# A two-layer state-space and expert kernel: the last y sums read from PSUM, the order behind the scans and its idle turns rewritten, expert rows added up by TensorE

## The reference

```python
x = x + _layernorm(_L0_attn_ref(_layernorm(x), ...))   # selective scan, 16 states
x = x + _layernorm(_L0_ffn_ref(_layernorm(x), ...))    # signs of x times signs of a weight
x = x + _layernorm(_L1_attn_ref(_layernorm(x), ...))   # the second selective scan
x = x + _layernorm(_L1_ffn_ref(_layernorm(x), ...))    # 16 experts, top 2, and a shared one
```

```python
scores = jax.nn.softmax(t @ gate_w.T, axis=-1)
weights, indices = jax.lax.top_k(scores, TOP_K)
for e in range(N_EXPERTS):
    w_e = jnp.sum(jnp.where(indices == e, weights, 0.0), axis=-1)
    y = y + _swiglu(t, w1[e], w3[e], w2[e]) * w_e[:, None]
z = _swiglu(t, sw1, sw3, sw2)
return y + z
```

## Time and profile before

| | us |
|---|---|
| median of 3 runs (lowest, highest) | 726.14 (725.17, 728.02) |
| the profiled execution | 727.01 |
| its span, from the first to the last instruction | 725.0 |
| TensorE, weight loads, VectorE, ScalarE, GpSimd busy | 627.7, 534.5, 559.0, 520.5, 443.9 |
| mean granted clock of TensorE | 0.927 of full speed |

### The profile page before, as it was taken

How to read it: one execution, slowest core, us unless ns; L and a number is a source line. 1 busy time by engine, 2 the same in 40 slices (tenths; PEclk the granted TensorE clock), 3 DMA queues, 4 the chain that set the end, 5 groups by cost and what they waited for, 6 DMA issues and landing times.

```text
span 725.0 us, 12906 instructions
## 1 busy us (share of the span) xinstructions
PE 627.7 (87%) x4302; PEld 534.5 (74%) x4303; DVE 559.0 (77%) x1068; ACT 520.5 (72%) x1267; POOL 443.9 (61%) x396
## 2 busy tenths in 40 slices
PE   4758999999994759489999999979899999999950
PEld 2348999999993423389999999977677677777630
DVE  6797999999997895879999999967832544344378
ACT  2959999999997969599999999963543222222425
POOL 0036999999997340369999999980674233333300
PEclk9957999999997869689999999999999999999985
DMA  6032454445440000144545454461122233332163
GB/s 182 5 73 76 143 147 133 143 140 145 135 145 1 0 2 7 42 111 135 160 127 161 135 154 140 133 206 46 66 103 94 88 102 102 108 108 95 64 219 116
DMA packets 57577, 77.83 MB, mean 107 GB/s; under 512 B 8112, under 2 KB 38480, under 8 KB 57520
## 3 DMA queue, kind: packets, MB, share of 16 engines
q1 hardware_dynamic: 53728, 66.75, 31.7%
q0 software_dynamic: 3792, 10.36, 4.0%
HBM read 58.21 MB, written 18.87 MB: 106 GB/s over the span
## 4 chain that ended last, share of the span: by engine, by line
PE 76%; DVE 11%; ACT 9%; DMA 2%; issue 1%; POOL 1%; ACTq 0%; SPq 0%; POOLq 0%; DVEq 0%
PE bank L1135 24%; PE bank L1158 15%; PE bank L1203 12%; PE bank L1137 4%; ACT tok_a L771 3%; PE bank L1048 3%; PE bank L1211 3%; PE bank L1212 3%; PE bank L1154 2%; DVE st L360 2%; DVE rings L740 1%; DVE arena L460 1%; PE bank L1273 1%; PE bank L1060 1%; PE bank L1074 1%
## 5 line engine op out<-in xcount | busy, mean ns | idle before, releaser
L961 POOL TENSOR_TENSOR arena<-arena,rings 128x512 f32<-128x512 f32 x256 | 317.2, 1280 | 23.2 <-DVE arena L557 22.0
L557 DVE TENSOR_TENSOR_SCAN arena<-rings,bank 128x512 f32<-128x512 f32 x256 | 302.1, 1211 | 14.1 <-PE bank L1137 12.3
L1135 PE MATMUL bank<-rings,tok_a 128*128 128x128 f32 x1536 | 217.9, 279 | 4.7 <-ACT rings L871 4.7
L1135 PEld LDWEIGHTS bank<-rings,tok_a 128*128 128x128 f32 x1536 | 196.4, 196 | 5.4 <-issue 5.4
L881 ACT ACTIVATE rings<-arena,a_sb 128x512 f32<-128x512 f32 x256 | 169.7, 709 | 1.1 <-DVE arena L557 1.1
L1158 PE MATMUL bank<-ident,arena 128*128 128x128 f32 x1024 | 152.4, 273 | 1.1 <-POOL arena L961 1.1
L871 ACT ACTIVATE rings<-ident,b_tok 128x128 f32<-128x128 f32 x384 | 124.5, 388 | 0.4 <-ACT tok_a L831 0.4
L1158 PEld LDWEIGHTS bank<-ident,arena 128*128 128x128 f32 x1024 | 119.4, 141 | 2.0 <-POOL arena L961 2.0
L1000 POOL DMA_INDIRECT y_tok<-rings,dest x47 | 45.5, 967 | 85.0 <-DVE rings L701 84.7
L936 ACT ACTIVATE silu<-bank 128x176 f32<-128x176 f32 x47 | 14.9, 318 | 85.7 <-PE bank L1203 85.7
L701 DVE COPY rings<-bank 128x256 f32<-128x256 f32 x47 | 20.0, 425 | 67.2 <-PE bank L1212 67.2
(11 more groups left out here) (170 smaller groups left out, 894.5 us busy)
## 6 DMA issues: line engine op xcount, KB each, us to landing
rings<-c_rows SPq DMA_DIRECT2D x128, 256.0 KB, 3.5
w_sb<-w SPq DMA_DIRECT2D x18, 352.0 KB, 4.3
x_sorted<-zeros SPq DMA_DIRECT2D x47, 128.0 KB, 3.4
rings<-x_sorted SPq DMA_DIRECT2D x47, 128.0 KB, 2.0
arena<-w SPq DMA_DIRECT2D x2, 2048.0 KB, 12.9
residual<-x SPq DMA_DIRECT2D x4, 512.0 KB, 5.8
tok_a<-y_tok SPq DMA_DIRECT2D x4, 512.0 KB, 7.9
w_sb<-y_tok SPq DMA_DIRECT2D x4, 512.0 KB, 9.1
```

The lines of the kernel that those rows point to most:

```text
L557: dve.tensor_tensor_scan(state[:, u % STATE_RING, :], abar[:, u % ABAR_RING, :], bank[u % B_RING][:, :], 0.0, ALU.mult, ALU.add).then_inc( ...
L961: pool.tensor_tensor(s, s, crep[:, k % CREP_RING, :], ALU.mult).then_inc(hc_ready, 1)
L1135: pe.matmul(o, tok_a[:, c, h * P:(h + 1) * P], v_ring[:, s % V_RING, j, 0:P], start=True, stop=True)
```

## The change

- SHARED_FIRST is 14: one more shared chunk ahead of the tiles, two behind.
- `y_last` is gone. Statistics and norm of the last y block read PSUM directly. The orders `first_y`, `first_f`, `last` and `combine` are rewritten. For the second layer's turns the target is banks 0 and 1, and turn 0 waits for the scan's last unit.
- The idle turns have other counts, with 16 new ones before turn 0 and 6 before the shared chunks.
- The picks of blocks 2 and 3 are one step. The second product of `expert_rows` takes the picks expert by expert, so that the copy that reordered its result goes; the multiply by 128 becomes part of the next addition; the first chunk's gated products come before the wait for the sums.
- ScalarE's function tables for silu and for the square root are loaded ahead of the first use.
- The weighted additions are TensorE's: `shared_part` puts `f_moe` into PSUM with the identity, `routed_part` adds each expert row through a diagonal of weights; the 32 diagonals are made by ScalarE (`mix_weights`), the first eight among the shared chunks, the others behind them. Statistics and norm read the sums in PSUM.

The diff, cut to its core:

```diff
-SHARED_FIRST = 13
+SHARED_FIRST = 14
...
+        turn_bank = [work, work, bank[0:2]]
+        mixed_in = [bank[6:8], bank[0:2], bank[2:4], bank[4:6]]
+        mix_diag = arena[:, 0:2 * C * P].rearrange("p (k c d) -> p k c d", k=2, c=C)
...
-        first_y = [("y_stat", 0), ("y_stat", 1), ("y_stat", 2), ("y_add", 0), ("y_last", 3), ("y_add", 1)]
-        first_f = first_y + [("f_stat", 0), ("y_add", 2), ("y_stat", 3), ("f_norm", 0)]
+        first_y = [("y_stat", 0), ("y_stat", 1), ("y_stat", 2), ("y_add", 0), ("y_add", 1), ("y_stat", 3), ("y_add", 2)]
+        first_f = first_y + [("f_stat", 0), ("f_norm", 0)]
         middle = first_f + [step for step in middle if step not in first_f]
-        last = first_y + [("y_stat", 3), ("y_add", 2), ("turn", 0), ("x_stat", 0), ("y_add", 3), ("turn", 1),
-                ("gate", 0), ("x_stat", 1), ("turn", 2), ("gate", 1), ("pick", 0), ("x_stat", 2), ("turn", 3),
-                ("gate", 2), ("pick", 1), ("x_stat", 3), ("gate", 3), ("pick", 2), ("pick", 3), ("x_norm", 0)]
-        combine = [("softmax", 0), ("gates", 1), ("m_add", 0), ("gates", 2), ("m_add", 1), ("gates", C - SHARED_FIRST),
-                   ("m_stat", 0), ("m_stat", 1), ("m_add", 2), ("m_norm", 0), ("m_stat", 2), ("m_norm", 1),
-                   ("m_add", 3), ("m_out", 0), ("m_stat", 3), ("m_norm", 2), ("m_out", 1), ("m_norm", 3),
-                   ("m_out", 2), ("m_out", 3)]
+        last = first_y + [("x_stat", 0), ("turn", 0), ("y_add", 3), ("turn", 1), ("x_stat", 1), ("gate", 0), ("turn", 2),
+                ("x_stat", 2), ("gate", 1), ("pick", 0), ("turn", 3), ("x_stat", 3), ("gate", 2), ("pick", 1),
+                ("gate", 3), ("pick", 2), ("x_norm", 0)]
+        combine = [("softmax", 0), ("gates", 1), ("gates", 2), ("m_stat", 0), ("m_norm", 0), ("m_stat", 1), ("m_norm", 1),
+                   ("m_out", 0), ("m_stat", 2), ("m_norm", 2), ("m_out", 1), ("m_stat", 3), ("m_norm", 3), ("m_out", 2),
+                   ("m_out", 3)]
+        def mix(c):
+            return mixed_in[c // CQ][c % CQ // 2][:, c % 2 * D:(c % 2 + 1) * D]
+        def last_y(c):
+            return ysum_of[(Q - 1) % 2][c % CQ // 2][:, c % 2 * D:(c % 2 + 1) * D]
...
-            def stat(src, q, ready=None, count=0, each=1):
+            def stat(src, q, ready=None, count=0, each=1, y_sum=False, mixing=False):
...
-                    done(dve.bn_stats(st6[:, c, :], src[:, c, :]))
+                    done(dve.bn_stats(st6[:, c, :], last_y(c) if y_sum else mix(c) if mixing else src[:, c, :]))
...
-                        if q == Q - 1:
-                            x_scales(q)
...
-                        stat(tok_a, q, last_y_copied, (l - 1) * 2, 2)
+                        dve.wait_ge(state_free, l * BATCH * UNITS)
+                        stat(tok_a, q, y_sum=True)
...
-                    dve.wait_ge(gate_ready, q + 1)
-                    done(dve.tensor_copy(gates[:, g, 0:E], logits[q]))
+                    if q == 1:
+                        x_scales(Q - 1)
+                    n = 1 if q < 2 else 2
+                    g = slice(q * CQ, (q + n) * CQ)
+                    for b in range(q, q + n):
+                        dve.wait_ge(gate_ready, b + 1)
+                        done(dve.tensor_copy(gates[:, b * CQ:(b + 1) * CQ, 0:E], logits[b]))
...
+            shared_gates(2)
             dve.wait_ge(prefix_ready, 1)
-            done(dve.tensor_copy(chunk_count, work[1][:, 0:C * E].rearrange("p (c e) -> p e c", c=C)))
-            settle()
-            done(dve.tensor_tensor_scan(chunk_end.rearrange("p e c -> p (e c)"), not_first,
-                                        chunk_count.rearrange("p e c -> p (e c)"), 0.0, ALU.mult, ALU.add))
-            shared_gates(2)
+            chunk_count = work[1][:, 0:C * E]
+            done(dve.tensor_tensor_scan(chunk_end.rearrange("p e c -> p (e c)"), not_first, chunk_count, 0.0, ALU.mult, ALU.add))
...
-            done(dve.tensor_scalar(row0[:, :], row0[:, :], float(P), None, ALU.mult))
-            settle()
-            done(dve.tensor_tensor(chunk_end, chunk_end, row0[:, :].unsqueeze(2).to_broadcast([P, E, C]), ALU.add))
+            done(dve.scalar_tensor_tensor(chunk_end, row0[:, :].unsqueeze(2).to_broadcast([P, E, C]), float(P), chunk_end,
+                                          ALU.mult, ALU.add))
...
-                elif name == "m_add":
-                    dve.wait_ge(moe_copied, (q + 1) * CQ)
-                    for j in range(CQ + 1):
-                        for k, c in ((0, q * CQ + j), (1, q * CQ + j - 1)):
-                            if not 0 <= c - q * CQ < CQ:
-                                continue
-                            if k == 0:
-                                dve.wait_ge(y_loaded[q], 16 * 2)
-                            else:
-                                dve.wait_ge(dve_done, steps[0] - (j < CQ))
-                            done(dve.scalar_tensor_tensor(f_moe[:, c, :], y_k[k][:, c, :], weights[:, c, k:k + 1],
-                                                          f_moe[:, c, :], ALU.mult, ALU.add))
-                    settle()
                 elif name == "m_stat":
-                    stat(f_moe, q)
+                    dve.wait_ge(mixed, q + 1)
+                    stat(None, q, mixing=True)
...
+                    y = last_y(c) if name == "y_add" and q == Q - 1 else mix(c) if name == "m_norm" else src[:, c, :]
+                    act.activation(dst[:, c, :], y, ACT.Identity, scale=rstd[:, c:c + 1], bias=shift[:, c:c + 1])\
...
+                    if (name, q, l) == ("x_stat", Q - 1, 2):
+                        act.preload_act_table_set("silu_and_others")
...
-                elif name == "y_last":
-                    act.wait_ge(state_free, l * BATCH * UNITS)
-                    for j in range(2):
-                        act.activation(tok_a[:, q * CQ + 2 * j:q * CQ + 2 * j + 2, :],
-                                       ysum_of[1][j][:, :].rearrange("p (c d) -> p c d", c=2), ACT.Copy).then_inc(last_y_copied, 1)
...
+            def mix_weights(q):
+                if q == 0:
+                    act.wait_ge(weights_ready, 1)
+                    act.wait_ge(ty_ready, TILES)
+                for c in range(q * CQ, (q + 1) * CQ):
+                    for k in range(2):
+                        ins = act.activation(mix_diag[:, k, c, :], ident[:, :], ACT.Copy, scale=weights[:, c, k:k + 1])
+                ins.then_inc(mix_ready, 1)
...
+                    if hi == C and c == lo:
+                        mix_weights(0)
...
+                        if c == C:
+                            act.preload_act_table_set("sqrt_and_others")
...
+            for q in range(1, Q):
+                mix_weights(q)
...
-            idle_turns = {("turn", 1): 14, ("gate", 0): 8, ("turn", 2): 12, ("gate", 1): 8, ("turn", 3): 12, ("gate", 2): 4,
-                          ("gate", 3): 8}
+            idle_turns = {("turn", 0): 16, ("turn", 1): 22, ("gate", 0): 2, ("turn", 2): 6, ("gate", 1): 4, ("turn", 3): 6,
+                          ("gate", 2): 4, ("gate", 3): 10}
...
-                    if l and q == 0:
-                        pe.wait_ge(last_y_copied, l * 2)
+                    if l == 1 and q == 0:
+                        pe.wait_ge(y_normed, C)
+                    if l == 2 and q == 0:
+                        pe.wait_ge(h_ready, 2 * BATCH * UNITS)
...
-                pe.wait_ge(onehot_ready, Q)
-                flat = picked.rearrange("p c e -> p (c e)")
-                pe.matmul(work[0][:, 0:C * E], upper_sb[:, :], flat, start=True, stop=True)
-                pe.matmul(work[1][:, 0:C * E], ones[:, :], flat, start=True, stop=True).then_inc(prefix_ready, 1)
+                pe.wait_ge(onehot_ready, Q - 1)
+                pe.matmul(work[0][:, 0:C * E], upper_sb[:, :], picked.rearrange("p c e -> p (c e)"), start=True, stop=True)
+                pe.matmul(work[1][:, 0:C * E], ones[:, :], picked.rearrange("p c e -> p e c"), start=True, stop=True)\
+                  .then_inc(prefix_ready, 1)
...
+                    if hi == C and c == lo:
+                        shared_part(0)
+                    if hi == C and c == C + 1:
+                        shared_part(1)
...
+            def shared_part(q):
+                for c in range(q * CQ, (q + 1) * CQ):
+                    pe.matmul(mix(c), ident[:, :], f_moe[:, c, :], start=c % 2 == 0, stop=False, skip_group_check=True)
+            def routed_part(q):
+                pe.wait_ge(mix_ready, q + 1)
+                pe.wait_ge(y_loaded[q], 16 * 2)
+                for k in range(2):
+                    for c in range(q * CQ, (q + 1) * CQ):
+                        ins = pe.matmul(mix(c), mix_diag[:, k, c, :], y_k[k][:, c, :], start=False, stop=k == 1,
+                                        skip_group_check=True)
+                ins.then_inc(mixed, 1)
...
+            stay_busy(6, bank[1])
...
+            shared_part(2)
+            routed_part(0)
```

(32 more changed lines are left out.)

3 lines of the change are left out of this document (1 added, 2 removed).

## The result

The changed kernel takes 725.01 us (median of 12 runs, lowest 723.59) against 726.67 us before (12 runs); the ratio is 0.9978, 95% interval 0.9968 to 0.9988. That is 1.7 us faster, where 4.4 were forecast. 725.0 lies inside the range, and the interval holds no 1, but the gain is under the 0.5% that I took for the smallest difference to be told: of a clear gain, little more than a third came. (One of the 12 runs of the changed kernel took 796.43 us in a slower state of the chip, and the ratio leaves it out.) The profiled execution took 725.35 us with a span of 723.5, against 727.01 and 725.0.

The account below looks back on a forecast made before the run. TensorE was taken to bound the middle stages, short VectorE instructions the routing, and a chain of loads, VectorE additions and a cold chunk the tail; -0.2 - 3.5 + 4.0 - 4.7 = -4.4 us, so 721.8 us, range 717.5 to 727.

Parts of the forecast that it names:

- Behind the first scan: First scan's end: dropping the 0.96 us copy of the last y sum gives -0.2 us, ends 1.0 gained and 0.3 lost.
- Turns, gates, picks, routing: Second scan to third shared chunk: no copy, fewer idle turns, shorter VectorE routing; -4.3 us at full clock, -3.5 taken.
- the warm end: Second scan to third shared chunk: with TensorE at full clock that chunk starts near 507.3, not 511.64, -4.3 us.
- Rival (d): Behind the second scan: idle turns, being transposes, do not hold TensorE's clock; up to 727.3 us, chance 0.03.
- I take -3.5, between the two, nearer to the warm end: Up to the third shared chunk: gain taken between -4.3 at full clock and 1.0 with clock falls and a late pick.
- Rival (a): Routing stretch: TensorE's clock falls from gate products or the new idle stretch; gain 1.0, not 3.5, 724.3 us, chance 0.25.
- signs of being wrong: Clock 0.5 within 683 to 712; routed product waiting over 1 us; chunk pitch other than 4.0; tiles starting after 563.
- One more chunk, paid in full: Ahead of the tiles: SHARED_FIRST 13 to 14 costs one chunk-loop pitch, +4.0 us, with POOL's scatters off the path.
- The tail: After the tiles: TensorE's sums replace VectorE's additions; 29.1 us plus 8.0 behind them, 37.1 instead of 41.8, -4.7 us.
- The 0.17 of the prediction: Tail: alternative estimate from the skill's fixed access cycles, four norms reading PSUM are 0.17 us shorter, not 0.4.
- Rival (b): Tail: bound by ScalarE or VectorE, roots and norms queueing behind 24 diagonals; tail 39.5 us, 724.2 us, chance 0.12.
- Rival (c): Tail: TensorE's sums run at half clock after a pause, 36 products at 0.86, +15.5 us, 737 us, chance 0.07.

Follow-up runs that it names:

- e7: Kernel before with only the last y sum's copy removed (statistics and norm read PSUM, second-layer turns in banks 0 and 1): 739.00 against 739.98 us, 0.9987.
- f4: Changed kernel without any idle turns, beside a kernel before of about 727 us: 732.41 us, ratio 1.0080.
- e1: Changed kernel plus 26 idle turns on TensorE ahead of the third shared chunk: 722.21 us, ratio 0.9944.
- e3: Changed kernel with SHARED_FIRST back at 13, so three shared chunks in the tail: 724.59 us, ratio 0.9968.
- f1: Changed kernel with 26 idle turns ahead of the third shared chunk, blocks 0 and 1 added by VectorE, SHARED_FIRST 13: 714.07 us, ratio 0.9821.
- e4: Changed kernel with additions split, blocks 0 and 1 on VectorE, blocks 2 and 3 on TensorE with 16 diagonals: 719.86 us, ratio 0.9900.
- e5: Changed kernel without any idle turns, on the chip where the kernel before took 740.0 us: 741.56 us, ratio 1.0016.
- e8: Changed kernel, 26 idle turns ahead of the third shared chunk, blocks 0 and 1 added by VectorE, SHARED_FIRST 14, chip of 740.0 us: 732.05 us, 0.9891.

## Why the prediction was wrong, step by step

**Behind the first scan**: right. -0.30 measured between the scan's last unit and the first f_turn, -0.2 forecast; e7 has the same with this edit alone.

**Turns, gates, picks, routing**: right in mechanism and size. Chunk 2 starts 4.16 us sooner, and -4.3 was the warm end. The routing's sums reach VectorE 3.0 us sooner behind the scan's last unit (3.2 forecast), and from there to chunk 2 are 5.91 us (5.8 to 5.9 forecast). Gates and first chunk ran at full clock, which is up to 1.7 us of the 4.16. Rival (d), that idle turns do nothing for the clock, does not hold: f4 shows what is lost without them.

**"I take -3.5, between the two, nearer to the warm end": this step failed.** I had named the new idle stretch of 3.2 us between chunks 1 and 2, priced a fall of the clock there at up to 1.75 us, and then took only 0.8 us off the warm end of -4.3. The stretch came (3.25 us) and cost 2.88: eight products 2.43 us longer, the three turns and the first down product behind them the rest. I had taken the price from the old first chunk, which ran cold for only a part of its products; a whole chunk cold is 5.0 us, as the old tail's already said. So the stretch up to chunk 3 gained 1.28 us and not 3.5. Rival (a) named this mechanism, with a chance of 0.25 and a gain of 1.0; e1 takes the idle stretch away and gets 722.2 us. That this is within 0.4 of the forecast is partly luck, since the 1.3 us that the tail fell short (below) are missing there too. Of the signs of being wrong that I had listed, only this came, as a first pitch of the chunk loop of 7.14 us in place of 4.0; I had named no window of the clock between the gates and the loop.

**One more chunk, paid in full**: right, +3.99, and the scatters stayed off the path. That the chunk costs nearly the same in the tail is e3; that it need not, f1.

**The tail**: the mechanism was right, the size was not. Forecast 29.1 + 8.0, measured 29.8 + 8.5, -3.4 in place of -4.7. The 48 products took 20.7 us, as forecast (20.6). The 0.7 lies in the work of the two last shared chunks: the first eight up products took 2.63 us and not 2.37 (0.3), the second group of turns 0.55 and not 0.33 (0.2), and the wait and rounding are the rest. VectorE came to the last sum 0.6 us late, at 715.56 in the chain, as forecast. The 0.5 lies behind that: from there to the end are 7.94 us and not 7.4, of which 0.3 is a norm that gains less from PSUM than the 0.4 I took and 0.2 the last store (2.77 us from VectorE's last addition to the end of the span, 2.56 before). The norms from PSUM in the changed kernel and from SBUF in the one before (the three figures are the least, median and greatest ns of one):

```profile
L769 ACT ACTIVATE rings<-bank,shift,rstd x16: 555/565/572, 705.7 to 719.4; 128x256 f32<-128x256 f32 x16
...
L771 ACT ACTIVATE rings<-rings,shift,rstd x16: 584/586/600, 709.1 to 721.1; 128x256 f32<-128x256 f32 x16
```

That is 565 ns against 586, and four take 1.93 us instead of 2.07, 0.14 less; no run shows the 0.4. The 0.17 of the prediction, an estimate worked out from the Trainium skill ("VectorE: DVE Perf Modes", the section on the TRN2 errata), was the better number. Rival (b), a tail bound by ScalarE or VectorE, does not hold: the diagonals were done at 705.1, TensorE waited 0.6 us in 29.8, and e4, which takes 24 products off TensorE and gives VectorE the additions of two blocks, gained 5.2 us. Rival (c) did not happen: the clock was full until TensorE was done.

Against my own sum, the two errors are 2.2 us before the tiles and 1.3 in the tail, 3.5 of the 4.4. That would leave -0.9, and the two traces have -0.83 behind the point where the edits begin. The medians of the runs say -1.7; the other 0.8 us no run assigns.

## What to carry to other kernels

When work ahead of TensorE gets shorter, look at the pauses that this opens in TensorE's own queue, and price a fallen clock over everything that runs until it comes back, not over one old case. One trace is not enough to say where it falls: the kernel before and e7 had the same wait of 2.60 us and their falls in different chunks. A move of additions from one engine to TensorE is worth only what the other engine bound; here 20.7 us of products replaced 15 us of VectorE for 1 us, and a split over both engines gave 5.2 us more and left room to hide a chunk.

## What the runs showed that I had not expected

A busy TensorE is not one at full clock: in f4 it is busy for 5.00 of 5.00 us at 0.50 during the gate products, and transposes that nobody reads, put before and between them, go with 1.00 and 7.4 us less in the changed kernel. The clock can also fall with no idle stretch in front. In the kernel before TensorE was busy for 14.00 of 14.00 us with turns, idle turns and gate products, and then it fell:

```profile
485.00:499.00 14.00, 14.00 (x131) 14.00 (x129) 9.65 (x69) 6.66 (x16) 2.75 (x5) 1.00 0.54 170
499.00:500.00 1.00, 1.00 (x6) 0.77 (x6) 0.62 (x4) 0.00 (x0) 0.00 (x0) 0.74 0.00 0
```

In e7, with the same counts of idle turns, the clock did not fall there, and in the ten traces with the new counts it did not either. No run settles what decides it.

On the chip of e5 to e8 all kernels, the one before too, took longer (the one before 740.0 us and not 726.8; the three others that ran on both chips 9 to 15 us more). In the trace of e8 the time lies in the shared chunks during GpSimd's scatters. Two rows of its timeline, TensorE and ScalarE:

```profile
546.35 2.71 PE L1235 MATMUL bank<-w_sb,feat_a 128*128 128x352 f32 x4 [6.86 <-issue]
...
552.45 0.41 ACT L938 ACTIVATE silu<-bank,x_scale 128x176 f32<-128x176 f32 x1 [6.59 <-remote]
```

TensorE stood for 6.86 us with nothing that the trace shows as a reason ("issue"), ScalarE for 6.59 until something outside the engines ("remote"), with more such waits around them, the first near 535. TensorE's long one ended at 546.35 with scatters still to come, ScalarE's at 552.45, 2.5 us behind the last of them (548.95 to 549.91); the chunks behind that ran without such a wait. The scatters themselves ran at their usual pace. Which queue held the two engines up, and why on this chip alone, no run here settles. e5 (1.0016) and f4 (1.0080) are one kernel on the two chips; that what comes earlier is partly lost in this stall would explain the difference. The traces bear it out in part: from chunk 3 to the first tile are 48.8 us in the changed kernel, 63.7 in e8 and 59.4 in e5, whose chunk 3 starts 8.8 us later than e8's and whose first tile only 4.5 later. The kernel before has no trace from this chip, so that this is the whole of the difference is argued and not shown.
